# A decoder layer with a routed mixture of experts: products of zeros in the routing stage, tags moved to VectorE, one chunk gathered there

## The reference

```python
x = layernorm(x + self_attention(x))            # 16 heads, ALiBi bias, causal, 128 tokens a sequence
x = layernorm(x + cross_attention(x, ctx))
x = layernorm(x + experts(x))

def experts(x):                                  # E = 8 experts, top K = 2, cap = ceil(1.2 * N / E) = 1229
    probs = softmax(x @ Wr + br)
    gates, ids = top_k(probs, 2)
    # sort by (expert, -gate); per expert the first `cap` (token, gate) pairs are its list
    xg = x[disp_tok].reshape(E, cap, D)
    h = silu(einsum('ecd,edh->ech', xg, W1) + b1)    # hidden 1024
    out = einsum('ech,ehd->ecd', h, W2) + b2
    return zeros.at[disp_tok].add(out * disp_gate)
```

## Time and profile before

| | before |
|---|---|
| median of 3 runs | 1590.31 us (1590.01 to 1591.07) |
| profiled execution, its own time | 1590.29 us |
| its span | 1588.6 us |
| mean granted clock of PE | 0.946 |
| PE busy | 1422.3 us, 90% |
| DVE busy | 1017.0 us, 64% |
| ACT busy | 1008.8 us, 64% |
| POOL busy | 619.9 us, 39% |

### The profile page before, as it was taken

How to read it: one execution, slowest core, us unless ns; L and a number is a source line. 1 busy time by engine, 2 the same in 40 slices (tenths; PEclk the granted TensorE clock), 3 DMA queues, 4 the chain that set the end, 5 groups by cost and what they waited for, 6 DMA issues and landing times. The chain is left out here.

```text
span 1588.6 us, 43802 instructions
## 1 busy us (share of the span) xinstructions
PE 1422.3 (90%) x17886; PEld 1197.1 (75%) x17886; DVE 1017.0 (64%) x2263; ACT 1008.8 (64%) x1504; POOL 619.9 (39%) x688
## 2 busy tenths in 40 slices
PE   8999999999999999999999772158999999999990
PEld 5777777777777777777777551048999999999980
DVE  5666666666677777777777647874454454454582
ACT  5677777767777776777777554246565565565563
POOL 2645444454542313222232100013455455455386
PEclk9999999999999999999999986558999999999995
DMA  6012222121122222222221173003443443443464
GB/s 194 28 56 62 62 62 62 49 64 54 61 62 68 82 69 74 75 82 82 82 81 42 55 219 86 0 8 103 97 104 48 99 102 50 99 103 50 95 241 180
DMA packets 115142, 130.72 MB, mean 82 GB/s; under 512 B 26650, under 2 KB 97084, under 8 KB 114944
## 3 DMA queue, kind: packets, MB, share of 16 engines
q1 hardware_dynamic: 100288, 106.18, 21.7%
q0 software_dynamic: 14656, 21.74, 7.8%
HBM read 83.73 MB, written 44.16 MB: 81 GB/s over the span
## 5 line engine op out<-in xcount | busy, mean ns | idle before, releaser
L527 ACT ACTIVATE at_pr<-at_A 128x2048 f32<-128x2048 f32 x128 | 240.8, 1881 | 147.0 <-PE at_A L347 147.0
L622 DVE TENSOR_REDUCE at_mx<-at_A 128x12 f32<-128x1536 f32 x128 | 224.6, 1755 | 55.8 <-PE at_A L312 52.2
L767 POOL TENSOR_SCALAR_AFFINE_SELECT at_pr<-at_pr 128x2048 f32<-128x2048 f32 x64 | 128.7, 2010 | 204.8 <-ACT at_pr L527 204.7
L1855 POOL DMA_INDIRECT total<-ex_o,ids x70 | 116.0, 1656 | 187.7 <-DVE ex_o L1783 172.8
L1724 DVE TENSOR_TENSOR ex_hT<-ex_h,ex_hT 128x384 fp32r<-128x384 f32 (+1 forms) x192 | 113.0, 588 | 95.8 <-ACT ex_hT L1657 95.5
L658 DVE TENSOR_TENSOR at_oT<-at_C,at_oT 128x512 fp32r<-128x512 f32 x64 | 44.3, 692 | 165.0 <-ACT at_oT L540 165.0
L347 PE MATMUL at_A<-at_qp,at_kt 32*128 32x256 f32 x2048 | 139.7, 388 | 0.0
L362 PE MATMUL at_C<-at_pr,at_v 128*32 128x128 f32 x4096 | 138.3, 276 | 1.0 <-ACT at_oq L534 1.0
L362 PEld LDWEIGHTS at_C<-at_pr,at_v 128*32 128x32 f32 x4096 | 104.0, 109 | 43.3 <-issue 42.1
L1656 ACT ACTIVATE ex_h<-ex_U,ex_b 128x384 f32<-128x384 f32 (+1 forms) x192 | 116.1, 605 | 29.8 <-PE ex_U L35 24.8
L774 POOL TENSOR_SCALAR at_shift<-at_mv 128x2 f32<-128x2 f32 x64 | 14.8, 230 | 265.0 <-DVE at_mv L686 262.4
(11 more groups left out here) (246 smaller groups left out, 3072.2 us busy)
## 6 DMA issues: line engine op xcount, KB each, us to landing
ex_w_in<-in_w SPq DMA_DIRECT2D x16, 1024.0 KB, 6.5
at_turned<-in_x_turned SPq DMA_DIRECT2D x16, 512.0 KB, 4.6
at_x<-in_x SPq DMA_DIRECT2D x16, 512.0 KB, 4.1
x<-at_y SPq DMA_DIRECT2D x32, 256.0 KB, 2.4
at_x<-x SPq DMA_DIRECT2D x16, 512.0 KB, 4.0
at_turned<-in_ctx_turned SPq DMA_DIRECT2D x16, 512.0 KB, 4.9
rows<-at_y SPq DMA_DIRECT2D x32, 256.0 KB, 2.3
total<-at_y SPq DMA_DIRECT2D x32, 256.0 KB, 3.0
```

Of the source, the lines that this page charges most:

```text
L527: nc.scalar.activation(pr[:, k % 2].rearrange("p i n a q -> p (i n a q)"), A[:].rearrange("p i n a q -> p (i n a q)"), ACT.Exp).then_inc(e ...
L622: nc.vector.tensor_reduce(mx[:, k % 2, 0:12], A[:, 0:3].rearrange("p i n a k -> p (i n a) k"), AX, ALU.max).then_inc(max_done, 1)
L767: nc.gpsimd.affine_select(out=t, in_=t, compare_op=ALU.is_ge, fill=0.0, base=0, pattern=[[0, 16], [1, P]], channel_multiplier=-1).then_inc ...
L1855: nc.gpsimd.indirect_dma_start(sum_dram, bass.IndirectOffsetOnAxis(ap=ids[0:n, e, at:at + 1], axis=0), o[0:n, pr, b, :], None, bounds_chec ...
```

## The change

Four things change.

- `iota8` gets a buffer outside the block and is loaded in `logits_block`. The two casts and DVE's wait for the other nine constants stand behind the writing of `runs`. PE waits for `tried` once before the search.
- PE gets products of zeros into a bank that nobody reads, `keep_busy(n)`: n products of 512 float16 columns with `ones_h` as weights. 16 stand behind the transposes of the slots, 4 behind each batch of the lists, 34 more behind the last batch, 12 behind the transposes of chunk 0. POOL clears `zeros_h` at the block's start.
- `ACT_TAGS` is (2,) and `DVE_TAGS` the other seven.
- `ROUTED` is 1.

```diff
-    ACT_TAGS = (0, 2, 4)
-    DVE_TAGS = (1, 3, 5, 6, 7)
+    ACT_TAGS = (2,)
+    DVE_TAGS = (0, 1, 3, 4, 5, 6, 7)
...
+        zeros_h = sb("zeros_h", [P, G], FP16)
+        idle_bank = c.enter_context(nc.psum_tensor("rt_idle", [P, G], FP32))
...
         def _(pe):
-            pe.wait_ge(const_in, 160)
+            def keep_busy(times):
+                for _ in range(times):
+                    nc.tensor.matmul(idle_bank[:, :], ones_h[:], zeros_h[:], start=True, stop=True)
+
+            pe.wait_ge(const_in, 144)
...
             pe.wait_ge(cleared, 1)
+            pe.wait_ge(tried, 1)
             for i in range(STEPS):
...
             last.then_inc(pe_done, 1)
+            keep_busy(16)
 
             for b in range(Q // BATCH):
...
                 last.then_inc(batch_done, 1)
+                keep_busy(4)
+            keep_busy(34)
             pe.wait_ge(x_loaded[0], 16 * parts[0])
...
                 last.then_inc(sh["t_full"], 1)
+            keep_busy(12)
...
             link(v.tensor_tensor(pr[:], pr[:], wide(col[:]), ALU.mult))
-            dve.wait_ge(const_in, 160)
-            v.tensor_copy(limits_h[:], limits[:])
-            v.tensor_copy(same_h[:], same[:])
-
             link(v.tensor_reduce(gates[:, 0, :], pr[:], AX, ALU.max))
...
             ins.then_inc(routed, 1)
+            dve.wait_ge(const_in, 144)
+            v.tensor_copy(limits_h[:], limits[:])
+            v.tensor_copy(same_h[:], same[:])
             dve.wait_ge(pe_done, 1)
...
             nc.gpsimd.memset(ones_h[:], 1.0)
+            nc.gpsimd.memset(zeros_h[:], 0.0)
...
-ROUTED = 2
+ROUTED = 1
```

In `logits_block` SP gets one more load and waits for it:

```diff
-            sp.wait_ge(zeroed, 32)
+            sp.dma_start(iota8[:], iota8_dram).then_inc(zeroed, 16)
+            sp.wait_ge(zeroed, 48)
```

More of the change, by code:

```diff
@@ L850, in inputs_of_logits, with logits_block @@
     return inputs
-def logits_block(nc, tiles, rows_dram, sum_dram, inputs, logits):
+def logits_block(nc, tiles, rows_dram, sum_dram, inputs, logits, iota8, iota8_dram):
     groups = tiles // NB
@@ L973, in _, with route_block @@
             take(groups - 1)
-def route_block(nc, tiles, cap, logits, rows_dram, ids, sh, consts):
+def route_block(nc, tiles, cap, logits, iota8, rows_dram, ids, sh, consts):
     LT = -(-cap // P)
@@ L1012, in route_block @@
         ebase = sb("ebase", [P, 1])
-        iota8 = sb("iota8", [P, E])
         gt = sb("gt", [P, F])
@@ L1082, in _ @@
         def _(sp):
-            for dst, name in ((ident, "ident"), (same, "same_expert"), (before, "before"), (ebase, "ebase"), (iota8, "iota8"),
+            for dst, name in ((ident, "ident"), (same, "same_expert"), (before, "before"), (ebase, "ebase"),
                               (iota_row, "iota_row"), (tag, "tag"), (part_base, "part_base"), (dummy, "dummy_row"), (limits, "limits")):
@@ L1101, in _ @@
             nc.scalar.activation(pr[:, :, :], pr[:, :, :], ACT.Exp).then_inc(act_done, 1)
-            act.wait_ge(const_in, 160)
+            act.wait_ge(const_in, 144)
             nc.scalar.activation(warm[:, 1:2], dummy[:], ACT.Sign)
@@ L1935, in decoder_layer @@
         logits = c.enter_context(nc.sbuf_tensor("logits", [P, tokens // P, E], FP32))
+        iota8 = c.enter_context(nc.sbuf_tensor("iota8", [P, E], FP32))
         with ExitStack() as near:
@@ L1940, in decoder_layer, with moe @@
                              {k: ins["xattn_" + k] for k in ("wq", "wk", "wv", "wo", "bq", "bk", "bv", "bo")}, ins, inputs)
-            logits_block(nc, tokens // P, rows, total, inputs, logits)
-        moe(nc, tokens, cap, ins, rows, total, out, logits)
-def moe(nc, tokens, cap, ins, rows, total, out, logits):
+            logits_block(nc, tokens // P, rows, total, inputs, logits, iota8, ins["iota8"])
+        moe(nc, tokens, cap, ins, rows, total, out, logits, iota8)
+def moe(nc, tokens, cap, ins, rows, total, out, logits, iota8):
     tiles = tokens // P
@@ L1949, in moe @@
         sh = shared_by_route_and_experts(nc, c, cap)
-        route_block(nc, tiles, cap, logits, rows, ids, sh, ins)
+        route_block(nc, tiles, cap, logits, iota8, rows, ids, sh, ins)
         experts_block(nc, tiles, cap, rows, ids, sh, total, out, {k: ins[k] for k in ("w1", "w2", "b1", "b2")}, ins)
```

## The result

The changed kernel takes **1599.2 us** (median of 4 runs, 1597.59 to 1601.49), against 1590.69 before in the same measurement: a ratio of 1.0048, 95% interval 1.0035 to 1.0061. It is slower. The forecast was 1585.8 and the range ended at 1594.5: wrong in sign and in size.

What follows compares the result with a forecast made beforehand. It took the routing stage between attention and experts, a chain every engine waits for with PE at half clock, as the bound; 2.07 + 0.1 + 2.35 = 4.5 us off 1590.29 gave 1585.8 us, range 1581.5 to 1594.5.

Steps and rivals of the forecast that it cites:

- Part 1: Start of the routing block: DVE no longer waits for constants before its reduction; 2.07 us gained.
- Part 2: Lists: retagging and zeros on PE, end of batch 7 at 1063.5 against 1063.64 before; 0.1 us gained.
- I take 0.103: Lists on PE: a list product at 2.4 GHz takes 0.103 us, so a batch takes 1.65 us.
- The bound of 0.156: Lists on PE: a list product at 2.4 GHz takes at most 0.156 us, its pace at 1.2 GHz.
- the twin: Kernel's start: 512-column products of zeros, first 0.43 then 0.21 us apart, taken as guide to zeros and list products.
- The clock falls in the 4.1 us gap: Lists, between batches 1 and 2: PE idles 4.1 us waiting for ACT's tags and likely drops to half clock.
- Regained after some 5 us of the mixture: Lists from batch 2: list products alternating with zeros restore full clock after some 5 us; 2.0 us lost.
- Rival B: Lists: clock falls in the gap before batch 2, the mixture doesn't raise it; batch 7 ends 1070.8, total 1593.7; 35%.
- rival A: Lists: the clock never falls, the 4.1 us gap does no harm; lists end 1061.5, total 1583.8 us; 20%.
- Part 3: From the lists' end into the first expert, with one routed chunk: 2.35 us gained, bounds 1.0 and 3.2.
- Zeros behind the lists: Between lists and chunk 0's transposes: 38 products of zeros take 8.0 us beside the gathers, cost nothing, leave 1.9 idle.

Runs made afterwards that it cites:

- iota_only: Kernel before with only `iota8` loaded a block earlier and the constants' wait moved later; 1590.82 us, ratio to before 0.9983 to 1.0001.
- bridged: Changed kernel with 30 products of zeros ahead of the lists instead of 16, DVE tagging all eight batches and two routed chunks; 1587.89 us.
- contig: Changed kernel with sixteen extra products per batch, their weights side by side, in place of the four zeros behind each batch; 1599.62 us (one run).
- act_filler: Changed kernel without any zeros, plus twelve one-column copies at the head of ScalarE's stream of the first expert; 1584.9 us.
- best_zeros: Changed kernel with DVE tagging all batches, two routed chunks, zeros only behind the last batch (34) and chunk 0's transposes (20); 1582.27 us.

## Why the prediction was wrong

**Part 1, the wait for constants, was right**: 2.07 forecast, 2.11 measured in iota_only and 2.12 in the changed kernel.

**Part 2, the lists: "I take 0.103", the price of a list product at 2.4 GHz, is the step that failed.** It is 0.153 at full clock (bridged) and 0.154 at half. The bound of 0.156 was in the text, but only the range's slow side knew it, and there only together with a lost clock. I had reasoned from the weight load of the twin at the kernel's start, 147 ns at first and 98 later (the twin's pace doubles between the two, but the windows there give a granted clock of 1.00 for both, so even this wasn't a reading of the clock); a list product's load takes 148 at either clock. That I never asked: whether this load, and not the twin's, follows the clock. The load of the zeros did here too (139 on average in the changed kernel, 107 in bridged), the list products' did not. Nor is the product simply as long as its load, as I took it to be: in contig 21 ns off the load took 7 off the product.

The Trainium skill ("TensorE: Matmul & The Clock Gate", LDWEIGHTS) puts the load at the number of columns over 1.2 GHz, an estimate of 107 ns for 128. The zeros' load met it at full clock (107 in bridged), the list products' at neither (148).

**"The clock falls in the 4.1 us gap" had the right kind of event in the wrong place.** There was a gap ahead of batch 0 that I had closed on paper: I let the 16 zeros last 6.9 us or nearly, to 1035 or 1037. They lasted 4.87 on the profile, since the clock rose in the middle of them, and left 3.42 us idle; the clock fell 1.1 us into batch 0 (0.57 in the window 1037 to 1038). In bridged, where PE has no such gap, it didn't fall.

**"Regained after some 5 us of the mixture" was wrong**: 30 us of it (1038 to 1068.6) at half clock never raised it. In the terms of my sum the lists went wrong by 7 us: six batches at 2.47 in place of 1.65 are 4.9, five times four zeros at 1.68 in place of 0.86 are 4.1, of which 2.0 were priced; 1063.5 + 4.9 + 2.1 = 1070.5. Rival B had this, and its end of the lists came out: 1070.8 forecast; 1068.6 + 2.1 = 1070.7 on the old scale. Its place for the fall did not (it had the later gap), and its 1593.7 is 3.9 below the profiled execution's 1597.59, close to the 4.4 by which Part 3 was off. Yet bridged shows that the same mixture, denser and at full clock, holds it. Raising and holding are two questions, and I had treated them as one. And with the clock held the zeros would still have cost 5 us: rival A, at 20%, was wrong too, for the price of the product.

**Part 3, one routed chunk: 2.35 gained was forecast, 2.0 lost were measured** (28.64 us from chunk 0 to `down` against 26.63 before). PE's own steps were near: the experts' first instruction came 3.80 us after the transposes (1078.62 to 1082.42, on DVE; 3.6 to 3.7 forecast), chunk 1's transposes 6.21 after it (6.06), with 1.63 us of waiting (1.7). The two together gained 2.43 us, where 2.66 were forecast. The two kernels with one routed chunk in which ACT had no idle times, act_filler and contig, reached `down` 24.1 and 24.7 us after chunk 0's transposes; 26.6 less 2.35 is 24.3. What failed is the unwritten term "ACT keeps up": its idle times of 4.6 us stood in no row of the trace before, and took the gain and 2 us more; why ACT stood idle stays open. No rival had it.

**Zeros behind the lists**: 8.0 us beside the gathers were forecast. They took 9.70, the first ones at half clock, and still ended 0.37 us before the rows were there.

## What to carry over

Before paying for a clock, ask of each kind of product whether it has a pace to gain: look for it, and for its weight load, at the other clock; here zeros between products that no clock speeds up made TensorE the bound, 8 us lost. Put zeros only where the engine has a wait of known length, make them fill it to the end, and end them at work whose pace follows the clock (best_zeros: 24 products in 4.45 us in place of 5.78). When a step is brought forward, list every engine that must keep up with it, the ones without idle time before included.

## What the runs showed of the hardware

- A product with 128 x 128 weights and 80 columns of float16 took 0.153 us at 2.4 GHz and 0.154 at 1.2; a product of zeros with 512 columns took 0.22 and 0.42 (four in 0.88 and 1.68 us); in bridged and the changed kernel.
- Weights that lie 16 elements apart took 148 ns to load at 1.2 and at 2.4 GHz, those side by side 127 at 1.2, the ones of the zeros 107 at 2.4.
- Batches of 2.45 us of such products with 0.88 us of zeros between them held the full clock for 26 us; the same with 1.68 us of zeros at half clock didn't raise it in 30 us.
- ScalarE stood idle for up to 3.1 us at one instruction, 4.6 to 6.3 us in all behind its entry into a block in eight kernels, with its inputs ready, and for 2.28 us with the DMA engines a third busy; the profile puts it down to the last engine that had signalled, or to "remote". With twelve small instructions ahead it was gone in one kernel and stood in three others; its cause is not shown.
